# RWKV-style attention and top-1 mixture of experts on one core: R squared up by VectorE, solve in 32x64 tiles, PE and SP queues reordered

## The chip, the cores and the metric

One Trainium2 chip, one of its cores. The metric is the device time of one execution in microseconds (us). The kernel before took 1094.39 us, the median of three runs (1082.82 to 1096.72). Everything is fp32 apart from a few routing tables in bf16.

## The reference, cut to what matters

The input is x of 8 sequences, 512 tokens, 256 channels. The attention layer has 16 heads of 16 channels. Per token it makes, by small and large projections, r, w, k, v, kk, a and a gate g, and runs a delta-rule recurrence per head:

```python
def step(s, inp):
    q_, w_, k_, v_, a_, b_ = inp
    sa = jnp.einsum('bhij,bhj->bhi', s, a_)
    s = s * w_[:, :, None, :] + sa[..., None] * b_[:, :, None, :] + v_[..., None] * k_[:, :, None, :]
    return (s, jnp.einsum('bhij,bhj->bhi', s, q_))
...
x = _layernorm(x + attention(x))
x = _layernorm(x + moe(x))      # 8 experts, 256 -> 1024 -> 256, argmax routing
```

## The kernel before, in words

The recurrence is done in NBLK = 16 blocks of 32 tokens. Inside a block, `scores` (line 646) makes the products of keys and reads, a unit triangular 32x32 matrix per head and sequence has to be inverted, `read_state` (lines 676, 682) gives the right-hand side R and the first part of the output in the PSUM banks `ry0` and `ry1`, `solve` (line 699) multiplies the inverse with R, `update` (716) and `read_out` (728) give the new state and the rest of the output.

256 matrices of a block are inverted on GpSimd (POOL), two halves of 128 partitions packed into one tile, in `invert` (lines 1896, 1903, 1906), one block after the other. They travel through DRAM by SP's queue: `scores_to_pairs(m)` stores the masked scores (scr_n, line 462) and reads them back with a matrix in each partition (467); when POOL is done, `inverse_to_heads(m)` stores the inverse (scr_u, 475) and reads it back in four pieces into `Ux` (486). SP's queue works in order, so each piece waits behind what stands ahead of it. In a body it issues: four loads of tokens (`load_tokens`, 444), the inverse (475, 486), the next input (423), the scores (462, 467), four stores of results (`store_x1`, 452).

The program is software-pipelined by hand: `body(n)` of each engine works on blocks n+2 (first low-rank step), n+1 (projections, decays, keys, scores), n (transposed keys and values, first read of the state), n-1 (R, solve, state, output) and n-2 (normalisation, gate, output projection, token statistics), and n-3 (router logits). Each engine has its own written order. PSUM is shared out by a `Ring`: a list of jobs with the bank of each (`"z@1"`), where a job waits (`wait_empty`) until the readers of the job before it in its bank are done, as named in `freed`. A `Stage` is a semaphore whose values count the steps of an engine, in the written order.

In the kernel before the path of R is: VectorE writes R twice, masked by head parity, into `Rm` (`keep_r`, line 1499, two products of 512 columns); TensorE transposes it (`turn_r`, eight transposes, line 654); ScalarE copies the result into `RT` (`keep_rt`, line 1148, two copies); TensorE multiplies in 64x64 tiles (`solve(m, f)`, 32 matmuls for each half f of the channels), where `Ux` holds the inverse with the other head's places zero; ScalarE and VectorE each copy one half of each result into `XV` (`keep_x` line 1153, `keep_x_odd` line 1505).

PE's body, in order and with lines: R part of read_state (676, 682), keys turned (654), hidden (595), k (561), keys, decay_a_kk (607: z, then a and kk), a filler matmul (769), router and gates (561), ma_mk (607), turn_r (654), project_out (561), solve(1) (699), norms, r (561), keys, v, solve(0) (699), keys and values turned (654), read_out (728), bonus (561), update (716), read_out (728), scores (646), gate_1 and low_1 (561), update, scores, centre_y, read_state, low_2 (579), variance_y, turn_x1. An fp32 matmul leaves two records in the trace, a transpose one.

DVE's chain that ends with the masked keys: keep_r (1499), sum_kk (1411), gated (1529), sum_decays (1391), key_gain (1397, 1399), add_tokens (1539), gain_keys (1415), token_stats (1545 to 1549), keep_x_odd (1505), key_exponent (1403, 1405), normed_kk (1452), decay_reads (1443), decay_kk (1474), removal (1458), decay_keys (1420), bonus_terms (1425), keep_x_odd, mask_removal (1467), mask_keys (1436). `scores` waits for the last of these. ACT feeds it: keep_z and keep_a (1009), keep_logits (1196), sigma_of_z, keep_ma, abs_of_z, keep_rt (1148), square_kk, sigma_of_abs, keep_mk, a table load (1015), log_sigma (1097), log_norm (1101), invert_norm (1122).

After the 16 blocks come the routing and 39 expert blocks, which the change does not touch.

## Time and profile before

| | |
|---|---|
| median of three runs | 1094.39 us (1082.82 to 1096.72) |
| profiled execution, its own time | 1087.63 us |
| its span, first to last instruction | 1085.4 us |
| TensorE clock granted, mean over the span | 0.974 |
| attention blocks | POOL's first inversion starts at 51.6 us, the last of the 16 at 679.4 |

The profile is of one execution. A row of the timeline gives start, duration, engine, line, operation, output and inputs, and how many records were merged; in brackets how long the engine had been idle before it and who ended that. PE is TensorE's matmuls, PEld its weight loads, DVE VectorE, ACT ScalarE, POOL GpSimd, SPq the DMA issues of SyncE. "issue" is idle time for which the profile shows no wait. PEclk is the granted clock as a share of the full one.

### The profile page before, as it was taken

Reading aid. Unit: us, or ns where it says so; the run is one execution under the profiler, and the core shown is the slowest. Engines: PE = TensorE matmul, PEld = TensorE weight load, DVE = VectorE, ACT = ScalarE, POOL = GpSimd, SP = SyncE. Lnnn points to the kernel's source line nnn. Section 1 sums busy time; section 2 is a strip of 40 time slices with the busy share of each in tenths; the row PEclk is TensorE's granted clock in tenths of the full one; section 3 lists DMA queues with packets and bytes.
Section 4 is the critical chain, followed back from the end, with each engine's and each line's share of the span. In section 5 each row is a group of like instructions: output and inputs, shape, how many; then the busy total and the mean of one; then the engine's idle time right before and its main releaser. Section 6 shows DMA issues by size and latency. Waiting matters only on the chain.

```text
span 1085.4 us, 42536 instructions
## 1 busy us (share of the span) xinstructions
PE 1010.8 (93%) x16804; PEld 833.9 (77%) x16805; DVE 777.0 (72%) x1777; ACT 542.0 (50%) x1113; POOL 614.4 (57%) x1135
## 2 busy tenths in 40 slices
PE   8898999999999999999999999499899999999995
PEld 5676777787777787777777777477799888989894
DVE  4776788788887887888788777157467666666663
ACT  4475677686685685776766766122122222222220
POOL 1088786787687885876867868820223232333321
PEclk9999999999999999999999999689999999999998
DMA  4113224234134133243242242828555454545430
GB/s 110 42 20 79 72 43 99 58 56 110 40 73 109 27 86 87 37 99 82 41 100 59 54 101 44 234 63 289 182 182 181 148 185 150 189 144 182 150 125 4
DMA packets 208752, 112.15 MB, mean 103 GB/s; under 512 B 172364, under 2 KB 192080, under 8 KB 208208
## 3 DMA queue, kind: packets, MB, share of 16 engines
q1 hardware_dynamic: 202208, 100.90, 34.4%
q0 software_dynamic: 3744, 8.40, 2.3%
q8 instruction: 122, 2.00, 0.8%
q10 hardware_dynamic: 2640, 0.54, 0.3%
q14 instruction: 38, 0.31, 0.1%
HBM read 85.55 MB, written 26.08 MB: 103 GB/s over the span
## 4 chain that ended last, share of the span: by engine, by line
PE 78%; DMA 7%; DVE 6%; issue 5%; ACT 1%; SPq 1%; POOL 1%; DVEq 1%; POOLq 0%; ACTq 0%
PE bank L561 19%; PE bank L950 12%; PE bank L963 9%; PE bank L646 6%; PE bank L699 6%; PE bank L654 5%; PE ry L963 4%; PE bank L607 3%; PE ry L676 2%; PE ry L728 2%; PE bank L716 2%; DMA arena<-scr_n 2%; DMA scr_n<-arena 2%; DMA arena<-scr_u 2%; DVE arena L1489 1%
## 5 line engine op out<-in xcount | busy, mean ns | idle before, releaser
L1906 POOL TENSOR_TENSOR arena<-arena 128x30 f32<-128x30 f32 (+14 forms) x480 | 263.5, 549 | 37.6
L561 PE MATMUL bank<-arena 128*128 128x256 f32 (+2 forms) x992 | 266.5, 406 | 5.9 <-DVE arena L1405 2.5
L1903 POOL TENSOR_TENSOR arena<-arena 128x30 f32<-128x30 f32 (+14 forms) x480 | 249.9, 521 | 36.4
L561 PEld LDWEIGHTS bank<-arena 128*128 128x128 f32 x992 | 172.7, 196 | 50.9 <-issue 24.7
L950 PEld LDWEIGHTS bank<-arena 128*128 128x128 f32 x1248 | 146.9, 194 | 5.5 <-issue 2.7
L950 PE MATMUL bank<-arena 128*128 128x128 f32 x1248 | 147.4, 277 | 3.1 <-DVE arena L1812 2.5
L1489 DVE TENSOR_TENSOR arena<-bank,arena 128x512 f32<-128x512 f32 x128 | 79.5, 682 | 32.8 <-PE bank L646 32.8
L1293 ACT ACTIVATE arena<-arena 128x1 f32<-128x1 f32 x39 | 11.5, 295 | 177.2 <-DVE arena L1766 177.2
L963 PE MATMUL bank<-arena 128*128 x416 | 96.4, 385 | 0.0
L1937 POOL COPY arena<-arena 128x1 int32 (+1 forms) x39 | 7.1, 183 | 146.2 <-DVE arena L1830 146.2
L963 PEld LDWEIGHTS bank<-arena 128*128 128x128 f32 x416 | 76.9, 190 | 14.4 <-issue 4.8
L699 PEld LDWEIGHTS bank<-arena 64*64 64x64 f32 x2048 | 65.3, 140 | 24.2 <-issue 16.7
L654 PE MATMUL bank<-arena 128*128 128x128 f32 x560 | 80.9, 281 | 2.0 <-issue 0.9
L699 PE MATMUL bank<-arena 64*64 64x32 f32 x2048 | 68.5, 224 | 14.2 <-DMA arena<-scr_u 12.1
L654 PEld LDWEIGHTS bank<-arena 128*128 128x128 f32 x560 | 64.9, 143 | 19.3 <-issue 13.6
L646 PE MATMUL bank<-arena 32*128 32x64 f32 x2048 | 69.0, 275 | 9.4 <-issue 8.5
L1931 POOL DMA_INDIRECT arena<-scr_x,arena x39 | 41.2, 1056 | 61.1 <-POOL arena L1929 30.4
L646 PEld LDWEIGHTS bank<-arena 32*128 32x128 f32 x2048 | 63.8, 188 | 13.7 <-issue 11.5
L1380 DVE SCALAR_TENSOR_TENSOR bank<-bank,arena 128x256 f32<-128x256 f32 x128 | 56.1, 483 | 22.4 <-PE bank L579 22.4
L1896 POOL MEMSET arena<- 128x32 f32 x16 | 2.5, 157 | 121.1 <-DMA arena<-scr_n 121.1
L1812 DVE TENSOR_SCALAR arena<-bank,arena 128x128 f32<-128x128 f32 x156 | 44.0, 344 | 23.1 <-issue 18.0
L1939 POOL DMA_INDIRECT out_dram<-arena x39 | 39.8, 1021 | 34.9 <-DVE arena L1796 20.8
(174 smaller groups left out, 1799.2 us busy)
## 6 DMA issues: line engine op xcount, KB each, us to landing
arena<-in_W SPq DMA_DIRECT2D x47, 1024.0 KB, 5.0
scr_n<-arena SPq DMA_DIRECT2D x64, 128.0 KB, 3.0
arena<-scr_n SPq DMA_DIRECT2D x16, 512.0 KB, 3.9
scr_u<-arena SPq DMA_DIRECT2D x16, 512.0 KB, 2.9
arena<-scr_u SPq DMA_DIRECT2D x62, 128.0 KB, 2.8
arena<-in_xTp SPq DMA_DIRECT2D x32, 132.0 KB, 4.1
arena<-in_x SPq DMA_DIRECT2D x64, 64.0 KB, 2.1
scr_x<-arena SPq DMA_DIRECT2D x64, 64.0 KB, 2.5
```

What stands on the lines that cost most here:

```text
L561: mm = pe.matmul(ring.tile(m, name)[0:rows, to], lhsT, rhs, start=(i == 0), stop=(i == len(terms) - 1))
L646: mm = pe.matmul(ring.tile(m, f"sc{f}{p}")[:, b * 2 * TB:(b + 1) * 2 * TB], bkm[r, f * B + b, :], aq[m % 2][r, f * B + b].rearrange("p x t ...
L654: mm = pe.transpose(ring.tile(m, name)[:, i * P:(i + 1) * P], src, ident)
L699: mm = pe.matmul(ring.tile(m, f"x{f}")[x, at:at + 32], Ux[m % 2][x, f, p, k].rearrange("p h t -> p (h t)"), RT[f][x, k, 32 * p:32 * p + 32 ...
L950: mm = pe.matmul(hidT_ps[t // 4][:, (t % 4) * P:(t % 4 + 1) * P], W1[s][:, k, t * P:(t + 1) * P], xnT[:, k, :], start=(k == 0), stop=(k == ...
L963: mm = pe.matmul(y_ps[s][:, 0:D], hidT[s][:, t, :], W2f[:, bass.ds(e * (FT * D) + t * D, D)], start=(t == 0), stop=(t == FT - 1))
L1380: xm_ok.inc(m, f"{g}{h}", STT(out=part, in0=part, scalar=prm(f"maa{g}", h), in1=dx[:, h], op0=ALU.add, op1=ALU.mult))
L1489: score.inc(m, name, TT(sc[m % 2][:, f, p].rearrange("p k e x t -> p (k e) (x t)"), ring.tile(m, name)[:, :].rearrange("p (b n) -> p b n", ...
L1812: relu_dve.inc(str(t), nc.vector.tensor_scalar(hidT[s][:, t], hidT_ps[1][:, (t - 4) * P:(t - 3) * P], b1f[:, bass.ds(e * FT + t, 1)], 0.0, ...
L1903: inv_ok.inc(f"m{s}", TT(t, U[:, 0:s, s:s + 1].broadcast_to(shape), U[:, s:s + 1, s + 1:TB].broadcast_to(shape), ALU.mult))
L1906: inv_ok.inc(f"a{s}", TT(U[:, 0:s, s + 1:TB], U[:, 0:s, s + 1:TB], t, ALU.add))
L1931: nc.gpsimd.indirect_dma_start(out=xg[:, s], out_offset=None, in_=x_rows, in_offset=bass.IndirectOffsetOnAxis(ap=index, axis=0), bounds_ch ...
```

## The change

- R: VectorE transposes the 32x32 squares of R straight from `ry0` and `ry1` into `Rs` (two transposes of 256 columns). `Rm`, `RT`, turn_r and keep_rt are gone.
- The inverse lies in DRAM and in `Ux` by pairs of heads on 32 partitions, dense; four loads as before, of the same size. The solve multiplies 32x64 tiles: for each pair row w and bank a or b, one matmul of 32 rows of R gives both heads, and the wanted one is picked afterwards.
- keep_x: VectorE takes three products with a 0/1 mask (bank a even and odd, bank b odd, 64x512 each), ScalarE two scaled copies of 64x256 (bank b even).
- PE: gates ahead of decay_a_kk, a and kk ahead of z, ma_mk ahead of the router; solve(0) right behind project_out, then norms, then solve(1), all ahead of r. The second half waits for the first by a semaphore, `half_solved`.
- ACT: a ahead of z, logits behind abs. DVE: gated ahead of sum_kk; all three products of keep_x behind key_exponent.
- SP: the inverse's store goes out first in the body, the token loads behind it (while it lands), the x1 stores of the block before after the inverse's loads.
- The ring's banks are dealt anew: among others v1 moves from bank 4 to 3, ma to 4, g to 4, wo and ss to 0.
- One more load at the start (`head_mask`, 128x34). The four products that mask the keys (1436, 1467) are not touched by the diff.

```diff
-        Rm_flat = take(NB // 2 * P)
-        RT = [take(4 * P).rearrange("p (k n) -> p k n", k=4) for _ in range(HALF)]
+        Rs = take(NB * TB).rearrange("p (e g i) -> p e g i", e=2, g=NB // 2)
+        head_mask = take(TB + 2)
...
-        nd = nc.dram_tensor("scr_n", (HALF, PAIRS, 4, 2, 2 * TB, TB), F32, kind="Internal").ap()
+        nd = nc.dram_tensor("scr_n", (PAIRS, 4, HALF, 2, 2 * TB, TB), F32, kind="Internal").ap()
...
-        ring = Ring(banks, [(0, "bk00@5"), (1, "h@2 k@3"), (0, "bk01@2"), (1, "z@1 a@4 kk@5"), (-3, "logit@2"),
-                            (-2, "g@0"), (1, "ma@5 mk@2"), (-1, "rt0@3 rt1@4"), (-2, "wo@0"), (-1, "x1@1"),
-                            (1, "ss@0 r@4"), (0, "bk11@5"), (1, "v@2"), (-1, "x0@3"), (0, "bk10@5 v0@1 v1@4"),
+        ring = Ring(banks, [(0, "bk00@5"), (1, "h@2 k@3"), (0, "bk01@2"), (-2, "g@4"), (1, "a@5 kk@3 z@1 ma@4 mk@2"),
+                            (-3, "logit@3"), (-2, "wo@0"), (1, "ss@0"), (-1, "xa@1 xb@3"), (1, "r@4"),
+                            (0, "bk11@5"), (1, "v@2"), (0, "bk10@5 v0@1 v1@3"),
...
             def inverse_to_heads(m):
                 sp.dma_start(ud, Up[m % 2].rearrange("p r c -> p (r c)")).then_inc(u_out, 16)
                 if m == last:
                     load_tokens(last)
+                elif m and m - 1 < last - 1:
+                    load_tokens(m - 1)
                 sp.wait_ge(u_out, (m + 1) * 16)
-                for e in range(2 if m < last else 1):
-                    for h in range(2):
-                        at_row = 64 * (1 - e) + TB * h
-                        sp.dma_start(Ux[m % 2][at_row:at_row + TB, :, :, :, h, :], u_rows[e, h]).then_inc(u_in, 16)
+                for p in range(PAIRS if m < last else 2):
+                    sp.dma_start(heads_of(m, p), u_rows[p]).then_inc(u_in, 16)
             def body(n):
-                if has(n - 2) and n - 2 < last - 1:
-                    load_tokens(n - 2)
                 if has(n - 1):
                     inverse_to_heads(n - 1)
+                if has(n - 3) and n <= last:
+                    store_x1(n - 3)
...
-            def solve(m, f):
-                ring.wait_empty(pe, m, f"x{f}")
-                chain_act.wait(pe, m, f"rt{f}")
-                pe.wait_ge(u_in, (m + 1) * 64)
-                for k in range(B // 2):
-                    for p in range(PAIRS):
-                        for e in range(2):
-                            x, at = x_rows_of(e), k * P + 32 * p
-                            mm = pe.matmul(ring.tile(m, f"x{f}")[x, at:at + 32], Ux[m % 2][x, f, p, k].rearrange("p h t -> p (h t)"),
-                                           RT[f][x, k, 32 * p:32 * p + 32], start=True, stop=True)
+            def solve(m, w):
+                if w == 0:
+                    for bank in "ab":
+                        ring.wait_empty(pe, m, f"x{bank}")
+                    chain_dve.wait(pe, m, "re", "ro")
+                    pe.wait_ge(u_in, (m + 1) * 64)
+                else:
+                    pe.wait_ge(half_solved, m + 1)
+                for g in range(NB // 2):
+                    for turn in range(2):
+                        for i, bank in enumerate("ab"):
+                            e, r = (turn + i) % 2, pair_rows(2 * w + i)
+                            at = (w * NB // 2 + g) * 32
+                            mm[bank] = pe.matmul(ring.tile(m, f"x{bank}")[x_rows_of(e), at:at + 32],
+                                                 Ux[m % 2][r, g % 4, g // 4, e].rearrange("p h t -> p (h t)"), Rs[r, e, g, :],
+                                                 start=True, stop=True)
...
-            def keep_rt(m, f):
+            def keep_x(m):
+                ring.wait_full(act, m, "xb")
+                for h in range(2):
+                    chain_act.inc(m, f"xb{h}", A(solution_home(m, 1, 0)[:, :, :, i], solution(m, "xb", 0)[:, :, :, i], ACT.Copy,
+                                                 scale=own_head[x, h:h + 1]))
...
             def keep_r(m):
                 for e, name in enumerate("eo"):
-                    chain_dve.inc(m, f"rm{name}", TT(Rm[:, :, 1 - e], RY[e][:, :, 0, None, :].broadcast_to(shape),
-                                                     odd_even[:, None, :, None].broadcast_to(shape), ALU.mult))
+                    chain_dve.inc(m, f"r{name}", nc.vector.transpose(Rs[:, e], RY[e][:, :, 0]))
+            def keep_x(m, bank, e):
+                ring.wait_full(dve, m, f"x{bank}")
+                chain_dve.inc(m, f"x{bank}{'eo'[e]}", TT(solution_home(m, "ab".index(bank), e), solution(m, f"x{bank}", e),
+                                                         same_head[x_rows_of(e), None, None, :].broadcast_to([P // 2, 2, NB // 2, 32]),
+                                                         ALU.mult))
```

TensorE, before, from the keys turned behind k to the second solve of a middle body (line 607 is decay_a_kk and ma_mk, 654 transposes, 699 solve; matmuls as written, two records each):

```order
L654 MATMUL bank<-arena 128x128 x4
L607 MATMUL bank<-arena 128x256 x6
L769 MATMUL bank<-arena 128x256
L561 MATMUL bank<-arena 128x8 x4
L561 MATMUL bank<-arena 128x256 x2
L607 MATMUL bank<-arena 128x256 x4
L654 MATMUL bank<-arena 128x128 x8
L561 MATMUL bank<-arena 128x256 x4
L699 MATMUL bank<-arena 64x32 x32
```

The same place after (618 is decay_a_kk and ma_mk, 666 transposes, 714 solve, 572 the other projections):

```order
L666 MATMUL bank<-arena 128x128 x4
L572 MATMUL bank<-arena 128x256 x2
L618 MATMUL bank<-arena 128x256 x10
L789 MATMUL bank<-arena 128x256
L572 MATMUL bank<-arena 128x8 x4
L572 MATMUL bank<-arena 128x256 x4
L714 MATMUL bank<-arena 64x32 x32
L572 MATMUL bank<-arena 128x512
L714 MATMUL bank<-arena 64x32 x32
L572 MATMUL bank<-arena 128x256 x4
```

The eight transposes of turn_r are gone, the gates stand two matmuls ahead of a, kk and z, and both halves of the solve stand around norms.

VectorE, before, from the products of keep_r to the second copy of the solution (1499 keep_r, 1529 gated, 1505 keep_x_odd, 1403 and 1405 key_exponent, 1452 normed_kk):

```order
L1499 TENSOR_TENSOR arena<-ry,arena 128x8x64 x2
L1411 TENSOR_TENSOR arena<-bank,arena 128x512
L1529 SCALAR_TENSOR_TENSOR arena<-arena,bank 128x256 x2
...
L1549 BN_AGGR arena<-arena 128x2 x2
L1505 COPY arena<-bank 64x4x128
L1403 SCALAR_TENSOR_TENSOR arena<-arena 128x512
L1405 SCALAR_TENSOR_TENSOR arena<-arena,bank 128x512
L1452 SCALAR_TENSOR_TENSOR bank<-bank,arena 128x512
...
L1425 TENSOR_TENSOR arena<-bank,arena 128x512
L1505 COPY arena<-bank 64x4x128
```

The same place after (1506 keep_r, 1535 gated, 1510 keep_x, 1411 and 1413 key_exponent, 1460 normed_kk):

```order
L1506 STREAM_TRANSPOSE arena<-ry 128x256 x2
L1535 SCALAR_TENSOR_TENSOR arena<-arena,bank 128x256 x2
L1419 TENSOR_TENSOR arena<-bank,arena 128x512
...
L1555 BN_AGGR arena<-arena 128x2 x2
L1411 SCALAR_TENSOR_TENSOR arena<-arena 128x512
L1413 SCALAR_TENSOR_TENSOR arena<-arena,bank 128x512
L1510 TENSOR_TENSOR arena<-bank,arena 64x2x8x32 x3
L1460 SCALAR_TENSOR_TENSOR bank<-bank,arena 128x512
```

Three products stand between key_exponent and normed_kk, where before one copy stood ahead of key_exponent and one far behind normed_kk.

SP's DMA queue, before, one turn (467 scores read back, 452 x1 stores, 444 token loads, 475 inverse stored, 486 inverse read back, 423 next input):

```order
L467 DMA arena<-scr_n 128x1024
L452 DMA scr_x<-arena 32x2x256 x4
L444 DMA arena<-in_x 32x2x256 x4
L475 DMA scr_u<-arena 128x1024
L486 DMA arena<-scr_u 32x32x32 x4
L423 DMA arena<-in_xTp 128x8x33 x2
```

After (479, 487, 456, 498, 464, 435 are the same steps as 467, 475, 444, 486, 452, 423):

```order
L479 DMA arena<-scr_n 128x1024
L487 DMA scr_u<-arena 128x1024
L456 DMA arena<-in_x 32x2x256 x4
L498 DMA arena<-scr_u 32x32x32 x4
L464 DMA scr_x<-arena 32x2x256 x4
L435 DMA arena<-in_xTp 128x8x33 x2
```

The store of the inverse moves past eight issues, its loads past four.

## Rows read from the trace of the kernel before

**Rows 1.** The page: busy time, share of the span and instructions

```profile
PE 1010.8 (93%) x16804; PEld 833.9 (77%) x16805; DVE 777.0 (72%) x1777; ACT 542.0 (50%) x1113; POOL 614.4 (57%) x1135
```

**Rows 2.** POOL: starts of the inversions (first and last), then its timeline

```profile
L1896 POOL MEMSET arena<- x16: 154/158/162, 51.6 to 679.4; 128x32 f32 x16
...
511.36 0.16 POOL L1896 MEMSET arena<- 128x32 f32 x1 [5.98 <-DMA arena<-scr_n]
...
548.15 0.24 POOL L1906 TENSOR_TENSOR arena<-arena 128x30 f32<-128x30 f32 x1
```

**Rows 3.** Windows: stretch, busy PE, PEld, DVE, ACT, POOL, PEclk, DMA share, GB/s

```profile
506.25:548.85 42.60, 41.17 (x921) 32.79 (x921) 34.12 (x61) 29.58 (x56) 32.40 (x61) 0.96 0.31 68
533.54:537.00 3.46, 2.03 (x63) 1.92 (x64) 1.96 (x3) 2.49 (x5) 3.15 (x5) 0.99 0.02 5
537.00:540.30 3.30, 3.30 (x16) 2.64 (x13) 2.48 (x4) 0.70 (x3) 2.91 (x6) 0.50 0.00 0
...
168.30:634.60 466.30, 445.54 (x10121) 353.08 (x10120) 379.98 (x661) 325.26 (x606) 355.64 (x672) 0.99 0.33 71
```

**Rows 4.** Timeline of PE in the body from 506.25 to 548.85

```profile
506.25 1.09 PE L676 MATMUL ry<-arena 32*32 32x64 f32 x64
...
517.29 1.09 PE L654 MATMUL bank<-arena 128*128 128x128 f32 x8
518.22 1.89 PE L561 MATMUL bank<-arena 128*128 128x256 f32 x8
520.04 2.06 PE L699 MATMUL bank<-arena 64*64 64x32 f32 x64
...
533.63 0.89 PE L646 MATMUL bank<-arena 32*128 32x64 f32 x23
535.86 1.64 PE L646 MATMUL bank<-arena 32*128 32x64 f32 x41 [1.34 <-issue]
537.43 3.43 PE L561 MATMUL bank<-arena 128*128 128x256 f32 x8
```

**Rows 5.** Timeline of DVE in the same body

```profile
512.34 1.28 DVE L1499 TENSOR_TENSOR arena<-ry,arena 128x512 f32<-128x512 f32 x2
...
516.34 0.87 DVE L1529 SCALAR_TENSOR_TENSOR arena<-arena,bank 128x256 f32<-128x256 f32 x2 [1.66 <-PE bank L561]
...
520.22 0.69 DVE L1539 TENSOR_TENSOR arena<-bank,arena 128x512 f32<-128x512 f32 x1 [0.48 <-PE bank L561]
...
522.37 0.65 DVE L1505 COPY arena<-bank 64x512 f32<-64x512 f32 x1
...
524.50 0.70 DVE L1452 SCALAR_TENSOR_TENSOR bank<-bank,arena 128x512 f32<-128x512 f32 x1
...
529.08 0.68 DVE L1505 COPY arena<-bank 64x512 f32<-64x512 f32 x1 [0.47 <-PE bank L699]
...
530.88 1.93 DVE L1436 TENSOR_TENSOR arena<-arena 128x512 f32<-128x512 f32 x2
```

**Rows 6.** Timeline of ACT in the same body

```profile
512.95 0.84 ACT L1009 ACTIVATE arena<-bank,arena 128x256 f32<-128x256 f32 x2 [0.22 <-PE bank L607]
515.37 0.18 ACT L1196 ACTIVATE arena<-bank 128x16 f32<-128x16 f32 x1 [1.58 <-PE bank L561]
...
522.29 0.63 ACT L1097 ACTIVATE arena<-arena 128x512 f32<-128x512 f32 x1
```

**Rows 7.** Timeline of SP's DMA issues at the next body's start

```profile
550.01 0.34 SPq L467 DMA_DIRECT2D arena<-scr_n  x1
...
555.12 0.37 SPq L475 DMA_DIRECT2D scr_u<-arena  x1
557.81 2.22 SPq L486 DMA_DIRECT2D arena<-scr_u  x4
```

**Rows 8.** Timeline of PE: the solve of the next and of the last block

```profile
563.93 2.06 PE L699 MATMUL bank<-arena 64*64 64x32 f32 x64 [1.22 <-DMA arena<-scr_u]
...
724.63 3.92 PE L699 MATMUL bank<-arena 64*64 64x32 f32 x128
```

160 lines of the change are left out of this document (77 added, 83 removed), and 2 rows, old and new, of the table ring.

## The prediction

> **What bounds the kernel now.** I read the page first. PE is busy for 93% of the span, the next engine for 72% [rows 1], so the eye goes to PE; but a share says nothing of what an edit is worth in a stage. So I went on to the windows and the timelines.
>
> The 16 attention blocks take most of the time. POOL starts its first inversion at 51.6 and its last at 679.4 us [rows 2]: 627.8 / 15 = 41.9 us for a block. Eleven middle bodies, from 168.30 to 634.60, take 466.30, so 42.39 each, with PE busy for 445.54 [rows 3]: 20.76 / 11 = 1.89 us idle in a body. I follow one body, from 506.25 to 548.85, and give places in it as offsets from 506.25.
>
> On PE the first half of solve starts at 13.8, right behind project_out, and scores at 27.4 [rows 4]. In the scores there is a gap of 1.34 that no wait explains. From 537.00 to 540.30, just behind this gap, the granted clock is 0.50, which is 1.2 GHz of 2.4; ahead of it PE was busy for 2.03 of 3.46 us [rows 3]. The eight matmuls of gate_1 and low_1 that fell into it took 3.36 us (to 540.79), where the eight of project_out took 1.82 [rows 4]: 1.54 us lost.
>
> DVE is the engine to look at beside PE. Its last product of masked keys ends at 530.88 + 1.93 = 532.81, offset 26.6 [rows 5], 0.8 ahead of the scores that wait for it. From add_tokens at 14.0 to there I find one wait of 0.47 between the rows shown, so this stretch is nearly full; it is fed by ACT, whose logarithm ends at 522.92, offset 16.7 [rows 6]. So PE has about 0.8 us in hand over DVE at the scores. What is taken off PE ahead of the scores beyond that turns into a wait, unless DVE's own chain gets shorter too.
>
> The third loop is POOL's. An inversion takes from 511.36 to 548.39, 37.0 us, and ahead of it POOL had waited 5.98 for the scores' loads [rows 2]. Its result was ready at 548.39 but SP stored it only at 555.12, behind the x1 stores and token loads; the loads of it were issued from 557.81 [rows 7] and PE waited 1.22 us for them at 563.93 [rows 8]. In most other bodies this wait is small.
>
> **PE, ahead of the scores.** Eight transposes go: they occupy 517.29 to 518.22, 0.93 us [rows 4]. Each half of solve holds 64 records. In 64x64 tiles they take 522.03 - 520.04 = 1.99 us, 31 ns each. For 32x64 tiles the trace has no row. The nearest ones are these 31 ns and the 32x32 tiles of read_state, 64 records in 1.09 less about 0.1 of drain, some 15 ns [rows 4]. The new shape has four tiles in turn instead of two, so I take 16 ns, 1.0 us per half; the bounds are 0.9 and 2.0. Both halves together save 2.0 us. The clear first half starts at 13.8 - 0.93 = 12.9, ends at 13.9, norms (two records of 512 columns, half the columns of project_out's 1.82) takes 1.0 with its start, and the second half ends at 15.9. With 0.93 + 2.0 saved PE would reach the scores at 27.4 - 2.9 = 24.5.
>
> **DVE and ACT.** keep_r is two products of 512 columns in 1.28 us [rows 5]; now two transposes of 256. No transpose on DVE is in this trace. Between nothing and 1.3 us each they change nothing behind them: DVE waited 1.66 us for the gate's bank [rows 5], and gated, now with its bank filled earlier, takes that place. I take 0.4 each, as a 256-column product of gated (0.87 for two). The Trainium skill gives a price: "VectorE: DVE Perf Modes", section "The three transpose paths", has 311 ns for a 128x128 bf16 transpose on VectorE, so for 256 columns an estimate of 0.62; the sum would be the same by it, since the slack covers it.
>
> What feeds DVE moves both ways. z's two copies began at 512.95, offset 6.7; two groups of matmuls now stand ahead of z (a with kk, and the gates, 1.0 each), so they begin at 8.7 and end at 9.5. Before, ACT then waited 1.58 for the logits [rows 6]; this wait goes, since a comes first. From the logits' end at 515.55 to the logarithm's end ACT needed 7.4 us. Less a's copies, which now stand ahead (0.7), keep_rt (0.5) and a wait of 0.6 for ma, plus the logits (0.2), 5.8 are left: the logarithm ends at 15.3, with a margin 15.5, 1.2 earlier. add_tokens follows project_out at 13.0 instead of 14.0; from it to keep_x_odd DVE took 522.37 - 520.22 = 2.15 [rows 5], to 15.2. key_exponent then runs from 15.5 to 17.0. Then come the three new products of 64x512: by the copy of the same shape 0.65 to 0.68 each, overlapped 1.9 in all, where one copy stood. normed_kk starts at 18.9, against 524.50, offset 18.25, before. From it to the end of the masked keys it was 532.81 - 524.50 = 8.3, with the second copy (0.6) and its wait (0.47) in it: 7.25 without. So the masked keys end at 26.2, with small hand-over delays 26.3: **only 0.3 earlier than before**. This is the term that decides. PE, ready at 24.5, waits about 1.8 us.
>
> ACT has 1.2 us of keep_rt and 1.2 of keep_x less, and two scaled copies of 64x256 more (0.4 each). v1's bank is now one that scores needs, so scores waits for ACT's copy of v1 too; with ACT lighter by 1.6 us I place its end at 25.7, 0.6 ahead of the masked keys. Where this cover is gone it costs what ACT is late.
>
> **Behind the scores.** From 533.63 to the next body's start it was 15.22, less the 1.34 gap and the 1.54 of low clock: 12.3. low_1 waits for the first kept score in its bank; DVE, now with its mix products behind the keys and the scores close behind them, reaches that 0.4 later in relation to PE. I take 12.7. A body free of disturbances is 26.3 + 12.7 = 39.0 (to 0.1).
>
> **Gaps and clock.** Of 1.89 us idle per body before, what falls ahead of the scores is swallowed by the new wait, what falls behind is not; the gap of this body starts in the scores. I keep 0.75 of it. Four of the eleven bodies show a stretch of low clock as in rows 3; with the new wait ahead of the scores I take one in 45 of 100 bodies, 0.7 us. Sum: 39.0 + 0.75 + 0.7 = 40.45, against 42.39: 1.94 less in a body.
>
> On the clock the Trainium skill speaks for the change: "TensorE: Matmul & The Clock Gate", section "HAM oscillation", has the throttle return in long idle waits, such as for DMA. By that rule a wait of 1.8 us costs nothing, and the sum would be 39.75 a body. The trace disagrees: 0.50 was granted behind a gap of 1.34 [rows 3].
>
> **SP and POOL.** The inverse's store passes eight issues: from 555.12 to 550.35 + 0.05, 4.7 us earlier [rows 7]. The token loads stand between it and its loads, but four of them took at most 2.7 us, and the store's landing, 557.81 - 555.12 = 2.7, covers them. Its loads then land about 8.8 us behind the store (issue at 557.81, wait ended at 563.93: 6.1 behind that), at offset 10.4 of the body after, against a solve that now needs them at 12.9. For shorter bodies this holds down to POOL's side: scores read back at 4.7 to 5.1, inversion 37.0, landing 8.8, is 50.9 from a body's start, and the solve is at 12.9 of the next: bodies shorter than 38.0 would wait. I count 0.2 us of waits won in the mean, already in the 1.94. x1 is needed only at the end; storing it later costs nothing while tokens' loads still come by 13.0, and they go out at about 2 to 5.
>
> **The sum.** Bodies 1 to 14 gain 14 x 1.94 = 27.2. Bodies -1 and 0 are padded with filler matmuls and wait for first inversions: nothing. In the last block 128 records of solve took 3.92 us [rows 8] and now about 2.0, but three products replace one copy behind it: 0.7 won. Routing and experts stay. 1087.63 - 27.9 = 1059.7 against the profiled execution's own time, which lies 6.8 below the median of the runs (1094.39). The saving off the median would be 1066.5. I say 1063.
>
> **Rivals.**
> *All of PE's saving counts.* If DVE's chain is not what scores waits for (its three products fit into holes, ACT is earlier than I place it), each body saves 0.93 + 2.0 + 0.2 = 3.1: 14 x 3.1 + 0.7 = 44, so 1044 to 1047. For it: PE is busy 445.54 of 466.30 [rows 3]. Against: the masked keys ended only 0.8 ahead of the scores, and three products now stand in front of them.
> *Nothing is won.* DVE's chain comes out 1 us longer (each product or the logarithm half a microsecond late, or the second half of solve still at 2.0 us, so that the first product waits for it at 17.9), and gaps and low clock stay: bodies of 41.7 to 42.2, 0.2 to 0.7 less: 1077 to 1091, say 1082. For it: DVE gets 0.6 us more work where it is full. This also covers the case that the change doesn't do what it says, tiles of 32x64 that overlap no better than 64x64.
> *Slower by the clock.* PE's new wait ahead of each scores brings low clock in each body, not in four of eleven, and it stays down while the scores and projections behind it run. One stretch costs 1.54. If three follow each other in a body, 39.0 + 0.75 + 4.6 = 44.4, 2.0 more than before: 1087.6 + 28 = 1116. It decides from two such stretches a body on (39.75 + 3.1 = 42.8). For it: rows 3. Against: gaps of 1.3 did this only in some bodies, and the stretch ended by itself after 3.3 us.
>
> **How the numbers follow.** Forecast 0.49, with a range of its own of 1052 to 1074; all of PE 0.17; nothing 0.26; slower by the clock 0.08. About 2% is what a measurement of this kernel tells from no change, here 1072.5 and 1116.3. Faster by more: 0.17 and 0.41 of the forecast's 0.49, 0.58. Within: 0.08 of the forecast's and 0.26, 0.34. Slower: 0.08. The range of 1042 to 1085 leaves out the clock's case and an edge on either side.
>
> **What would show it.** Right, if in the profile after: bodies of 40 to 41 us; the solve's 64 records in about 1.0 us; an idle time of PE of 1 to 2 us ahead of scores that the masked keys end; normed_kk at 18.9 behind R; SP's store of the inverse right behind the scores' load, and no wait for scr_u at solve. Wrong, if scores starts at 24.5 without a wait (then the time is near 1045), if 64 records still take 2.0 us, if another bank (v1, lo1) ends PE's waits, or if the low clock shows in each body.

## The result, and the profile after

The changed kernel took 1077.78 us (median of four runs, 1070.33 to 1079.46), the kernel before beside it 1093.45 (1082.82 to 1096.72): a ratio of 0.9876, 95% interval 0.9831 to 0.992. It is 1.2% faster, 15.7 us, where 1063 (2.8% under 1093.45) was forecast; the direction and the range held, the size did not. The profiled execution took 1079.2 us, span 1077.2, 8.2 less than before's span. It lies 1.4 above its median where before's lay 5.8 below its own, so the two traces show about half of the difference of the medians. In the comparisons below the ratios leave out executions more than 1.5% above the fastest of their kernel, while the medians include them, so that the two can differ by some us.

The page of the changed kernel, part 1, answers to [rows 1]:

```profile
PE 982.2 (91%) x16676; PEld 799.1 (74%) x16677; DVE 779.8 (72%) x1793; ACT 519.5 (48%) x1081; POOL 610.9 (57%) x1135
```

PE is busy for 28.6 us less, but the span fell by 8.2 only. The starts of the solves, which each block has one of, show where. In the table s1 is the solve of block 1, and so on; low clock is the sum of stretches with a granted clock of 0.50.

| stretch of the span | before | after | difference |
|---|---|---|---|
| start to s1 | 140.0 (low 3.4) | 143.2 (13.6) | +3.2 |
| s1 to s13, 12 bodies | 508.6 (13.6) | 491.0 (17.0) | -17.6 |
| s13 to s15 | 76.0 (27.3) | 76.8 (32.2) | +0.8 |
| s15 to first expert matmul | 47.3 (0.0) | 54.1 (15.6) | +6.8 |
| experts to the end | 313.5 (12.5) | 312.1 (9.3) | -1.4 |

The middle gained, 42.38 to 40.92 us a body, and both ends gave some of it back. Windows of the changed kernel, columns as in [rows 3] (the eleven middle bodies, then one of them):

```profile
172.30:620.50 448.20, 420.71 (x10037) 325.05 (x10039) 381.24 (x672) 309.87 (x584) 354.25 (x675) 0.98 0.34 74
499.50:540.60 41.10, 38.45 (x914) 30.04 (x913) 33.93 (x62) 28.13 (x54) 31.20 (x57) 0.96 0.35 74
```

Here a body has 40.75 us, PE is idle for 27.5 / 11 = 2.5 us of it, 0.6 more than before; DVE's work per body is the same as before (34.7 against 34.5 us). The body from 499.50, offsets from there. Timeline of PE, answering to [rows 4]:

```profile
509.85 2.78 PE L572 MATMUL bank<-arena 128*128 128x8 f32 x16
512.57 1.13 PE L714 MATMUL bank<-arena 32*64 32x32 f32 x64
513.63 1.12 PE L572 MATMUL bank<-arena 128*128 128x512 f32 x2
514.68 1.13 PE L714 MATMUL bank<-arena 32*64 32x32 f32 x64
...
522.53 1.10 PE L572 MATMUL bank<-arena 128*128 128x256 f32 x4 [0.62 <-DVE arena L1433]
523.72 0.75 PE L736 MATMUL bank<-arena 128*32 128x32 f32 x64
524.33 0.76 PE L748 MATMUL ry<-arena 128*32 128x32 f32 x64
526.99 2.30 PE L658 MATMUL bank<-arena 32*128 32x64 f32 x64 [1.91 <-issue]
```

Timeline of DVE, answering to [rows 5], and of ACT, answering to [rows 6]:

```profile
505.55 0.77 DVE L1506 STREAM_TRANSPOSE arena<-ry 128x256 f32<-128x256 f32 x2
506.24 0.87 DVE L1535 SCALAR_TENSOR_TENSOR arena<-arena,bank 128x256 f32<-128x256 f32 x2
...
516.40 2.00 DVE L1510 TENSOR_TENSOR arena<-bank,arena 64x512 f32<-64x512 f32 x3
518.33 0.68 DVE L1460 SCALAR_TENSOR_TENSOR bank<-bank,arena 128x512 f32<-128x512 f32 x1
...
523.49 1.70 DVE L1444 TENSOR_TENSOR arena<-arena 128x512 f32<-128x512 f32 x2
```

```profile
514.29 0.63 ACT L1116 ACTIVATE arena<-arena 128x512 f32<-128x512 f32 x1
```

A half of the solve gives way to norms, or to r, 1.06 us after its start, where it took 1.99. The two transposes take 0.77 us together, and gated follows with no wait. The logarithm ends at 514.92, offset 15.4, the masked keys at 525.19, offset 25.7 (26.2 is the median of the bodies). PE would be at the scores at 525.09, and had waited 0.62 for DVE on the way, in front of bonus (L1433 is DVE's product for it). So the two engines arrive together; then a gap that no wait explains puts the scores at offset 27.5.

SP's queue at the start of the next body (540.60), answering to [rows 7], and the waits of PE from 160 to 620 us, in groups (us in total, times, longest):

```profile
542.12 0.34 SPq L487 DMA_DIRECT2D scr_u<-arena  x1
542.55 2.63 SPq L456 DMA_DIRECT2D arena<-in_x  x4
546.17 2.24 SPq L498 DMA_DIRECT2D arena<-scr_u  x4
```

```profile
PE bank L572 <- DVE arena L1433: 8.2, 11, 1.1
PE bank L658 <- issue: 7.8, 10, 1.9
PE ry L694 <- issue: 3.4, 5, 1.0
PE bank L572 <- DVE arena L1497: 3.0, 5, 0.8
PE bank L658 <- DVE arena L1444: 1.6, 6, 0.4
...
PE bank L714 <- DMA arena<-scr_u: 0.8, 2, 0.5
```

PE waits for DVE in every body, for the most part one step ahead of the scores (0.7 us at bonus), and for the inverse almost nowhere.

The ends. Timeline of PE at the first solve and at the last ones, answering to [rows 8]; then the window of low clock around the last, and the one from there to the experts; last, the same stretch of the kernel before (s15 to the first expert matmul):

```profile
99.77 1.50 PE L714 MATMUL bank<-arena 32*64 32x32 f32 x48 [3.39 <-DMA arena<-scr_u]
...
675.58 3.94 PE L714 MATMUL bank<-arena 32*64 32x32 f32 x128 [5.97 <-DMA arena<-scr_u]
...
711.01 4.15 PE L714 MATMUL bank<-arena 32*64 32x32 f32 x128 [4.92 <-DMA arena<-scr_u]
717.36 1.83 PE L748 MATMUL ry<-arena 128*32 128x32 f32 x121 [2.19 <-DVE arena L1510]
```

```profile
709.50:726.60 17.10, 11.84 (x268) 9.63 (x269) 9.93 (x29) 3.31 (x9) 0.74 (x1) 0.50 0.31 85
726.60:765.12 38.52, 35.17 (x195) 28.63 (x193) 19.95 (x60) 4.79 (x10) 3.40 (x4) 1.00 0.72 263
```

```profile
724.63:771.92 47.29, 44.01 (x462) 35.77 (x461) 28.98 (x92) 8.46 (x19) 4.15 (x5) 1.00 0.67 240
```

And the solve of block 14 in the kernel before, a row that the prediction had not read:

```profile
690.00 7.04 PE L699 MATMUL bank<-arena 64*64 64x32 f32 x128 [9.73 <-DMA arena<-scr_u]
```

So both kernels wait for the inverse at the solve of block 14, 9.73 us before and 5.97 now. At that of block 15, PE came without a wait and at full clock before; now it is there sooner than the inverse, waits 4.92 us, and works at 0.50 up to 726.60: the 128 records take 4.15 us, in tiles that should be faster, where the old ones took 3.92.

Not all of this is POOL's own time. POOL's and SP's rows around the inverse of block 14, PE's in the scores of block 15, and windows of low clock there and behind the first solve:

```profile
664.32 0.24 POOL L1913 TENSOR_TENSOR arena<-arena 128x30 f32<-128x30 f32 x1
668.80 0.15 POOL L1903 MEMSET arena<- 128x32 f32 x1 [4.24 <-DMA arena<-scr_n]
```

```profile
664.59 0.44 SPq L514 DMA_DIRECT2D arena<-in_mats  x1
...
666.98 0.43 SPq L517 DMA_DIRECT2D arena<-in_b1T  x1
667.52 0.38 SPq L487 DMA_DIRECT2D scr_u<-arena  x1
```

```profile
649.33 1.44 PE L658 MATMUL bank<-arena 32*128 32x64 f32 x41 [1.36 <-issue]
...
653.07 3.69 PE L658 MATMUL bank<-arena 32*128 32x64 f32 x64
```

```profile
99.77:108.70 8.93, 8.93 (x138) 6.67 (x139) 4.77 (x7) 4.65 (x8) 7.93 (x13) 0.50 0.17 26
651.50:661.70 10.20, 10.20 (x261) 7.76 (x260) 6.37 (x12) 3.54 (x7) 8.87 (x18) 0.50 0.30 50
```

The inverse of block 14 is ready at 664.56, but its store goes out at 667.52, behind three loads for the routing that both kernels issue between these bodies (`load_routing`): 2.9 of the 5.97 us. And the last inversion starts late. Behind the gap of 1.36 us the granted clock was 0.50 for 10.2 us from 651.5, with PE busy throughout; the second half of the scores of block 15 took 3.69 us in it, and POOL could start on them only at 668.80, 34.6 us behind s13, where the kernel before took 30.8.

### The profile page after: what moved, and what is told of

It reads as the page before. It is cut to its first block, busy times and chain, and to the rows that moved or that the text cites. A ratio compares the mean times of both kernels' runs of the same rounds, so it can differ in the third digit from the quotient of the medians.

```text
span 1077.2 us, 42188 instructions
## 1 busy us (share of the span) xinstructions
PE 982.2 (91%) x16676; PEld 799.1 (74%) x16677; DVE 779.8 (72%) x1793; ACT 519.5 (48%) x1081; POOL 610.9 (57%) x1135
## 4 chain that ended last, share of the span: by engine, by line
PE 61%; DVE 12%; POOL 9%; DMA 8%; issue 7%; ACT 2%; SPq 1%; DVEq 1%; ACTq 0%; POOLq 0%
PE bank L572 14%; PE bank L969 12%; PE bank L982 9%; PE bank L658 5%; POOL arena L1913 5%; POOL arena L1910 4%; PE ry L982 4%; PE bank L714 3%; PE bank L618 3%; DMA scr_u<-arena 2%; DMA scr_n<-arena 2%; PE ry L688 2%; PE bank L666 2%; DMA arena<-scr_u 1%; DVE arena L1497 1%
## 5 line engine op out<-in xcount | busy, mean ns | idle before, releaser
L572 PE MATMUL bank<-arena 128*128 128x256 f32 (+2 forms) x992 | 274.9, 412 | 21.3 <-DVE arena L1433 10.8
L572 PEld LDWEIGHTS bank<-arena 128*128 128x128 f32 x992 | 174.1, 198 | 60.8 <-issue 19.6
L969 PEld LDWEIGHTS bank<-arena 128*128 128x128 f32 x1248 | 145.2, 192 | 5.8 <-issue 3.0
L969 PE MATMUL bank<-arena 128*128 128x128 f32 x1248 | 145.9, 275 | 3.2 <-DVE arena L1819 2.5
L1497 DVE TENSOR_TENSOR arena<-bank,arena 128x512 f32<-128x512 f32 x128 | 79.4, 681 | 24.5 <-PE bank L658 24.5
L982 PEld LDWEIGHTS bank<-arena 128*128 128x128 f32 x416 | 76.9, 190 | 14.4 <-issue 4.9
L658 PE MATMUL bank<-arena 32*128 32x64 f32 x2048 | 71.6, 282 | 12.4 <-issue 9.2
L658 PEld LDWEIGHTS bank<-arena 32*128 32x128 f32 x2048 | 66.2, 194 | 17.1 <-issue 15.3
L666 PE MATMUL bank<-arena 128*128 128x128 f32 x432 | 61.9, 278 | 3.6 <-DVE arena L1510 1.6
L666 PEld LDWEIGHTS bank<-arena 128*128 128x128 f32 x432 | 51.5, 143 | 18.0 <-issue 12.0
L714 PEld LDWEIGHTS bank<-arena 32*64 32x64 f32 x2048 | 37.9, 149 | 33.8 <-issue 23.8
L1316 ACT ACTIVATE arena<-bank,arena 128x128 f32<-128x128 f32 x156 | 44.5, 368 | 25.3 <-PE bank L969 25.3
```

Of the source, the lines that this page charges most:

```text
L572: mm = pe.matmul(ring.tile(m, name)[0:rows, to], lhsT, rhs, start=(i == 0), stop=(i == len(terms) - 1))
L658: mm = pe.matmul(ring.tile(m, f"sc{f}{p}")[:, b * 2 * TB:(b + 1) * 2 * TB], bkm[r, f * B + b, :], aq[m % 2][r, f * B + b].rearrange("p x t ...
L666: mm = pe.transpose(ring.tile(m, name)[:, i * P:(i + 1) * P], src, ident)
L714: mm[bank] = pe.matmul(ring.tile(m, f"x{bank}")[x_rows_of(e), at:at + 32], Ux[m % 2][r, g % 4, g // 4, e].rearrange("p h t -> p (h t)"), R ...
L969: mm = pe.matmul(hidT_ps[t // 4][:, (t % 4) * P:(t % 4 + 1) * P], W1[s][:, k, t * P:(t + 1) * P], xnT[:, k, :], start=(k == 0), stop=(k == ...
L982: mm = pe.matmul(y_ps[s][:, 0:D], hidT[s][:, t, :], W2f[:, bass.ds(e * (FT * D) + t * D, D)], start=(t == 0), stop=(t == FT - 1))
```

## The experiments

Theory A: the middle bodies gained what DVE and ACT's chain allows, and the rest was lost at both ends, where PE, now earlier, waits for the inverse and pays for it again by the clock. Theory B: the chain itself is longer than forecast. Theory C: it is chance, gaps that move with the program's code. Differences below are between medians unless said otherwise; each ratio is to the kernel before run beside it. Only the next four experiments (again, fillers, narrowed, SP's old order) ran beside the changed kernel; the others are set against it by way of their ratios.

**The changed kernel again.** 

> The changed kernel again, on the chip of the next three, so that they can be set against it. In its first profile a middle body took 40.75 us against 42.39 before, as the forecast's chain gives (scores start at 26.4 of the body, 26.3 was forecast); but the first two bodies were 3.2 us later and 6.6 us were lost between the last solve and the first expert block, where the clock was low for 17 us. Theory A (what was won in the middle is given back at the two ends, where PE waits for the inverse and the clock falls): the same again, 12 to 20 us faster than before, middle bodies 40.4 to 41.0. Rival B (that profile was an odd one; the ends cost nothing): 25 to 30 us faster.

Measured: 1079.89, ratio 0.9892 (0.9848 to 0.9937). Body 40.94, last solve to experts 54.9, and again low clock (13.7 us) in the scores of block 15, with the last inversion 36.9 us behind s13: what the first trace showed repeats. Its profiled execution took 1087.25, 7.4 above the median, so it shows the losses larger than they mostly are.

**Fillers at both ends.**

```diff
+                if n == 1 or n == last:
+                    ring.wait_empty(pe, n - 1, "xa")
+                    keep_busy(6 if n == 1 else 11, ring.tile(n - 1, "xa"))
                 if has(n - 1) and n - 1 < last:
                     solve(n - 1, 0)
...
-                    keep_busy(2, idle_ps)
+                    keep_busy(12, idle_ps)
...
+                if n == last + 1:
+                    keep_busy(4, route_ps)
```

> Filler matmuls where PE waits for the inverse: 6 ahead of the first solve, 11 ahead of the solve of block 14, 12 in place of 2 ahead of that of block 15, 4 behind it. Nothing that anyone waits for is made earlier. Theory A: the low-clock stretches at both ends go or shrink from about 50 us in all to under 25, the first two bodies come back by 1 to 2 us and the stretch from the last solve to the first expert block by 4 to 6: 4 to 8 us faster than the changed kernel. Rival C (the ends are late by the waits alone, the clock has no part in it): no change, or slower by up to 2 us through fillers that run over.

Measured: 1071.08, ratio 0.9822 (0.9778 to 0.9866), 8.8 less than the changed kernel beside it. Low clock behind s13 fell from 51.3 to 17.0 us, last solve to experts from 54.9 to 50.4. The work added is 31 matmuls, and yet the time falls. The two traces exaggerate, since that of this kernel is of its fastest execution (1065.55). Against the first trace of the changed kernel s1 comes 2.1 us earlier (141.1), s13 to s15 takes 1.7 less and the stretch to the experts 3.7 less, but 6.1 us stand in the twelve middle bodies (40.41 us each), in which the edit adds nothing. By the ratios the gain is 7.6 us.

**DVE's three products narrowed.** `keep_x` on DVE takes 4 of 32 columns in blocks 2 to 14; the rest of the masking is left out.

> VectorE's three products of keep_x take 4 of 32 columns in blocks 2 to 14, so the kernel leaves out most of the masking of the solution there; nothing else is moved. This takes about 1.4 us out of VectorE's chain ahead of the masked keys. Theory D (that chain is what scores waits for): the masked keys end 1.4 earlier, scores starts 0.5 to 1.0 earlier (then ScalarE's copy of v1, which ends at 25.9, or PE itself comes last), bodies 0.4 to 1.0 us shorter, 5 to 12 us in all. Rival E (PE's own work sets the body, its waits are only where it happens to pause): under 2 us.

Measured: 1067.73, ratio 0.9776 (0.9719 to 0.9833), 12.2 less. The three products take 0.61 us in place of 2.00, and the masked keys end at offset 25.3; the scores still start at 26.3 (26.4 in the changed kernel), now behind ACT's copy of v1, which ends at 25.8. Timeline of DVE in this kernel:

```profile
510.26 0.61 DVE L1511 TENSOR_TENSOR arena<-bank,arena 64x64 f32<-64x64 f32 x3
510.79 0.68 DVE L1460 SCALAR_TENSOR_TENSOR bank<-bank,arena 128x512 f32<-128x512 f32 x1
```

The middle bodies have 40.57 us, 0.35 to 0.37 less for 1.39 us taken out of the chain. So the chain is on the path, but ACT is close behind DVE, as the 0.6 us of cover in the prediction said, and only about 4 of the 12.2 us come from these bodies. In the profiles 3.3 to 5.0 us stand ahead of s1, where the edit changes nothing, and 3.8 to 6.0 between s13 and s15, where this kernel has no low clock ahead of the last inversion.

**SP's old order in the changed kernel; SP's new order alone in the kernel before.** In the first `load_tokens` is ahead of `inverse_to_heads` again, `store_x1` behind `scores_to_pairs`' loads; in the second the kernel before gets only SP's part of the diff.

> The changed kernel with SP's old order: x1 stores and token loads ahead of the inverse's store. Theory F (the new order is needed now, since the first solve stands 2 us earlier in the body than before): the inverse lands at about 15 of the body instead of 10.5, PE waits about 2 us at each solve, the second half ends at 18, keep_x and all behind it come 0.8 to 1.0 later: 10 to 16 us slower than the changed kernel, that is about as slow as before. Rival G (the inverse was never late by more than its 0.2 us in the mean): under 3 us slower.

> The kernel before with SP's new order and nothing else: the inverse's store goes out first, token loads behind it, x1 stores behind its loads. The undoing of it in the changed kernel cost 18 us, more than the 16 us that the whole change brings. Theory F (the new order is worth much only together with the earlier solve; before, PE waited for the inverse 0.2 us in a body and at three places at the ends): 2 to 7 us faster than before, from the waits of 9.7 and 1.2 us at the last blocks. Rival H (SP's order is the whole gain, the rest of the change brings nothing): 12 to 18 us faster than before.

Measured: the first 1098.21, ratio 1.0052 (1.0015 to 1.0089), 18.3 more than the changed kernel beside it by the medians and 17.5 by the ratios, bodies of 42.31; the second 1092.22, ratio 0.9997 (0.9964 to 1.003), bodies of 42.70. PE's waits of the first from 160 to 640 us:

```profile
PE bank L656 <- issue: 6.1, 8, 1.2
PE bank L712 <- DMA arena<-scr_u: 5.6, 5, 1.8
PE bank L712 <- issue: 4.3, 2, 3.2
```

The new order is worth all of the gain in one kernel and nothing in the other. Twelve bodies of 42.31 instead of 40.94 are 16.4 us. PE's waits for the inverse show 5.6 of them directly; 4.3 more at the solve have no wait that the profile shows. The delay runs on through the solve: the masked keys end at 27.6 of a body in the mean, where it was 26.3. Alone in the kernel before, the new order cut the wait at s14 from 9.73 to 6.38 us, but the 2 to 7 us that this was expected to bring did not come. Only where the solve stands earlier in the body does the inverse come last.

**z ahead of a and kk.** On PE and ACT, and in the order of the stage.

```diff
-                from_hidden(m, [[("a", 0, slice(64, 96), hid), ("kk", 0, slice(96, 128), kkh)]])
                 from_hidden(m, [[("z", 2, slice(0, P), hid)]])
+                from_hidden(m, [[("a", 0, slice(64, 96), hid), ("kk", 0, slice(96, 128), kkh)]])
```

> The changed kernel with z ahead of a and kk again, on TensorE and ScalarE. In the two bodies at the start, where no gates stand ahead, a and kk wait 0.4 to 0.8 us for ScalarE's copy of k (its bank is kk's now), and the first inversion starts at 53.1 instead of 51.6, the second at 92.6 instead of 90.3. Theory A: the first inversion starts at 51.6 to 52.0 again, the second at 90.5 to 91.5; in a middle body nothing changes, since ScalarE makes z and a one after the other: 0 to 3 us faster. Rival: the order of a and z sets ScalarE's logarithm, then bodies move by 0.5 us either way and the time by 6.

Measured: 1072.82, ratio 0.9855 (0.9805 to 0.9906). s1 is at 140.3, as before the change, and bodies have 40.23. In the changed kernel a and kk wait at the start for ACT's copy of k, since kk lies in k's bank; with z first they don't. PE of the changed kernel, and of this one:

```profile
55.27 1.98 PE L618 MATMUL bank<-arena 32*128 32x256 f32 x11 [0.40 <-ACT arena L1084]
```

```profile
53.65 2.09 PE L618 MATMUL bank<-arena 128*128 128x256 f32 x12
```

The wait is gone, and the first inversion starts at 52.1 instead of 53.1. How much of s1's 3.2 us it explains is not shown: s1 was at 143.2 and 144.9 in the two traces of the changed kernel, and at 139.9 in the kernel with the narrowed products, whose program is the same up to there. Most of the gain stands in the middle bodies, 0.7 us each, as the rival allowed and theory A did not: the logarithm ends 0.3 us earlier, at offset 15.2, and part is low clock, 6.8 us in the twelve instead of 17.0. The interval overlaps with those of the changed kernel (0.9831 to 0.992, 0.9848 to 0.9937).

**Fillers ahead of the scores.** Two, in the bank of the first score, in bodies 1 to 14.

> The changed kernel with two filler matmuls (0.92 us) ahead of the scores in the bodies 1 to 14, where PE waits for the masked keys. Theory D (PE waits there about 1 us in a body, split into 0.7 ahead of bonus and 0.3 ahead of scores): fillers that fit into what is left of the wait cost little, 0.3 to 0.6 us a body, 3 to 8 us slower, unless they keep the clock up; if a short wait there is what brings the low clock in the middle (17 to 24 us of it in two profiles), that falls to under 10 us and the two cancel: 3 us faster to 4 us slower. Rival E (PE sets the body): 0.92 us in each of 14 bodies, 13 us slower.

Measured: 1072.45, ratio 0.9837 (0.9789 to 0.9884), an interval that again overlaps with those of the changed kernel. Low clock in the middle 6.8 us, as expected; bodies of 40.75, which is 2 us less in twelve. That 0.92 us of fillers a body cost nothing rules out rival E, that PE's work alone sets the body.

**Router ahead of ma and mk, alone and with those fillers.** `router(n - 3)` and its filler stand ahead of `ma_mk(n + 1)` again.

> The changed kernel with the router (and the filler matmul ahead of it) back in front of ma and mk. Theory D (the chain z, ma, mk on ScalarE, logarithm, key_exponent, three products, masked keys sets the scores): ma's bank is filled 1.5 us later, ScalarE waits 0.7 us for it, the logarithm ends at 16.1 instead of 15.5 and the masked keys 0.6 later; bodies 0.4 to 0.6 us longer, 5 to 9 us slower. Rival E (PE sets the body): nothing, under 2 us.

> The changed kernel with router and its filler back ahead of ma and mk (which alone made bodies of 42.98 and 54 us of low clock in the middle), and two fillers ahead of the scores. If the clock amplifies a delay of ACT's chain (a longer wait ahead of the scores brings low clock), the fillers take most of the low clock away: bodies of 41.5 to 42.0, 10 to 14 us faster than router first alone, ratio 0.990 to 0.994. If the chain alone makes the bodies long, the fillers give nothing: bodies of 42.8 to 43.2, ratio 1.002 to 1.006.

Measured: alone 1096.39, ratio 1.0042 (1.0 to 1.0085), bodies of 42.98 with 54.4 us of low clock in the twelve; with the fillers 1085.75, ratio 1.0001 (0.9969 to 1.0033), bodies of 41.85 with 20.4. Alone, the logarithm ends 0.9 us later (offset 16.4), the body 2.1; PE's waits from 160 to 640:

```profile
PE bank L572 <- DVE arena L1433: 14.7, 11, 1.9
```

A delay of 0.9 in the chain made the wait at bonus 1.3 instead of 0.7 us a body. The clock can account for the rest: 54.4 - 17.0 = 37.4 us more at half speed are 3.1 in a body, which costs up to 1.6. The fillers shorten no chain, and in the profile they still took half of it back. How large the amplification is stays uncertain. The profile without fillers is of one of its longer executions (1099.23; four of the ten took 1086 to 1089), and the fillers won 4.5 us by the ratios, where 10 to 14 were expected; the two intervals overlap.

**Together, and in the kernel before.** The third has the fillers of the second experiment ahead of its solves, in the bank `x1`, without the four behind the last.

> The changed kernel with all three edits that each gave 7 to 9 us: z ahead of a and kk, two filler matmuls ahead of the scores in bodies 1 to 14, and the fillers at the first and the last two solves. If the three gain from different places (start and bodies, gaps of the bodies, end), they add up in part: period of the middle bodies 40.1 to 40.5, low clock to the last solve's experts under 20 us, last solve to first expert matmul 50 to 51 us; the time about 1060 to 1066, ratio 0.973 to 0.978. If they all only remove the same low clock, the best single one is the floor: 1068 to 1072, ratio 0.981 to 0.984.

> The changed kernel with z ahead of a and kk and the fillers at the ends, without the fillers ahead of the scores. If the fillers ahead of the scores cost bodies their own time (two matmuls of 0.47 us in a wait of 0.7 to 1.8 us) and give back only in bodies with low clock, this is equal to the kernel with all three, within 3 us. If the gaps ahead of the scores are what starts the low clock, it is 3 to 7 us slower than with all three.

> The kernel before with the same fillers at the ends (6 ahead of the first solve, 11 ahead of the solve of block 14, 12 in place of 2 ahead of the last). Theory: the changed kernel lost 6.8 us between its last solve and the experts to waits and low clock that the kernel before hasn't; there PE waited little, so fillers only stand in PE's way: 0 to 4 us slower than before, ratio 1.000 to 1.004. Rival: the fillers are a gain of their own that any kernel has, which says nothing of the change: 4 to 9 us faster, ratio 0.992 to 0.996.

Measured: all three 1074.65, ratio 0.9874 (0.9818 to 0.993); z and ends 1070.3, 0.9853 (0.9802 to 0.9904); the kernel before with fillers 1098.55, 1.0111 (1.0067 to 1.0155). Nothing adds up: bodies have 41.21 and 40.77 us, longer than with z first (40.23) or the end fillers (40.41) alone. The fillers are not a gain that any kernel has: before the change they cost 11 us, more than expected. From s14 to s15 there are 37.9 us instead of 34.6, since PE had no wait at s15 to fill; 6 us stand in middle bodies that the edit doesn't touch (42.86). The expectation was wrong to say that PE waited little there: it waited 9.73 at s14, and filling that gave nothing.

**Code moved, nothing else.** Five or ten matmuls of 8 columns more in body 0, ahead of a wait; and the fillers at both ends once more beside them.

> The changed kernel with five matmuls of 8 columns more (0.17 us each by the router's row) behind the fillers of body 0, where PE then waits 3.39 us for the first inverse anyway. They can change no body behind it but by moving the program's later code on in memory. If the gaps that the profile puts down to issue (7.8 us ahead of matmuls of the scores in eleven bodies) are set by where code stands, they fall in other places, and the period of the middle bodies leaves 40.92 by 0.2 to 0.6 us either way, the time by 2 to 8 us. Rival: the period is set by the chain of DVE and ACT alone: 40.8 to 41.0, time within 2 us of 1078 to 1080.

> The same with ten such matmuls. If code placement counts, the period of the middle bodies differs from that with five by 0.2 to 0.6 us, in no order that the number of matmuls explains; by the rival it is 40.8 to 41.0 again.

> The changed kernel with the fillers at its first and its last two waits once more, beside the two shifted kernels on one chip. If its 8.8 us came from the waits at the ends, it is again 50 to 51 us from the last solve to the first expert matmul with under 20 us of low clock there, and 6 to 10 us faster than the shifted kernels; if from a lucky placement of the middle bodies, the profile has the same 40.4 period (the code is the same) and the ends are where the difference isn't.

Measured: 1082.64, ratio 0.9936 (0.9905 to 0.9967), and 1082.88, ratio 0.9941 (0.9904 to 0.9978), with bodies of 41.00 and 40.91; the fillers 1069.99, ratio 0.9859 (0.9824 to 0.9895), with bodies of 40.48 and 49.3 us from last solve to experts. For these two shifts theory C falls for the body: the gaps ahead of the scores went from 7.8 us to 6.0 and 10.0, the period stayed. Both are 3 to 5 us slower than the changed kernel by the medians and 5 to 7 by the ratios; up to 4.4 of it stand ahead of s1 (145.0 and 147.6 for 143.2). The gain of the fillers holds: 12.7 us against the shifted kernels by the medians, 8.4 to 8.9 by the ratios. Timeline and window of its last solve:

```profile
699.23 5.34 PE L789 MATMUL bank<-arena 128*128 128x256 f32 x24
704.50 2.35 PE L714 MATMUL bank<-arena 32*64 32x32 f32 x128
706.78 1.99 PE L789 MATMUL bank<-arena 128*128 128x256 f32 x8
```

```profile
704.50:753.80 49.30, 43.98 (x469) 35.48 (x468) 29.70 (x89) 8.11 (x19) 4.14 (x5) 1.00 0.65 232
```

No wait, full clock, and 2.35 us for the 128 records that took 4.15. With a ratio of 0.9822 and 0.9859 in its two comparisons it is the best confirmed version; z first (0.9855) and the fillers ahead of the scores (0.9837) can't be told from it. Its interval overlaps a little with that of the changed kernel beside it the first time, and not with those of the two shifted ones.

## Why the prediction was right and wrong

- *The solve, 1.0 us a half for 2.0*: right. The pitch from one half to the next step is 1.06, which is 17 ns a record.
- *DVE's transposes, 0.4 each, without effect*: right, 0.77 for both.
- *ACT's chain, logarithm at 15.5; products 1.9; normed_kk at 18.9; masked keys at 26.3*: right to 0.3: 15.5, 2.0, 19.15, 26.2 in the median. This was the term called decisive. Narrowing the products made the bodies 0.35 us shorter, delaying the logarithm made them longer.
- *PE waits 1.8 us ahead of the scores*: half right. PE waits for the same chain one step earlier, at bonus, 0.7 us a body, and arrives at offset 25.6 in the body shown, not 24.5. I had put no name to that step's input, DVE's product behind normed_kk.
- *A body of 40.45*: nearly, 40.92 between solves. Behind the scores 14.3 us stood where 12.7 + 0.75 + 0.7 = 14.15 was summed; another part is gaps ahead of the scores, as the 1.91 in the body shown, which I had let the wait swallow. So 1.46 us was gained, not 1.94: 12 x 0.48 = 5.8 us of the miss.
- *Bodies 1 to 14 gain 14 x 1.94*: **the step that failed**, together with the two terms for the ends that follow. The steady gain was carried over to the whole pipeline. Twelve bodies gained. From s13 to s15 the kernel got 0.8 us slower, where 2 x 1.94 was counted, 4.7 us of the miss: these solves wait for the inverse, 5.97 and 4.92 us. The sentence on POOL's side said that bodies shorter than 38.0 us would wait, and was used for the steady state alone; the last bodies have no next block to project, and from s14 to s15 there were 34.6 us already before. A part is the clock and not the change of pace: in the traces of changed kernels where 0.50 was granted around the scores of block 15, s13 to s15 took 75.8 to 79.0 us, in the others 71.5 to 75.1, against 76.1 before.
- *Bodies -1 and 0: nothing*: wrong, +3.2 us. The moved a and kk need a bank that ACT still holds; PE waits, the first inversion starts 1.5 us later, and the first solve waits 3.39 us, with the clock at 0.50. Putting z first took the wait for the bank away; that it also gave back all of the 3.2 is not shown, since s1 moved as much between kernels with the same program up to there.
- *In the last block 0.7 won*: wrong, 6.8 us lost up to the experts, 7.5 of the miss and its largest term. 2.35 us, not 2.0, is what 128 records cost at full clock, and here they ran at half of it. It had 15.6 us of low clock in this stretch, the kernel before none.
- *The sum off the median*: the terms give 28 us, 15.7 were measured. (1063 itself is the mean of this sum off the profiled execution and off the median, and lies 3.5 below the latter.) In the traces the four misses above, 5.8, 4.7, 3.2 and 7.5, make 21.2 of 27.9. The profiles show 17.6 in the middle, and +3.2, +0.8, +6.8 and -1.4 elsewhere, which is 8.2 in sum; the other 7.5 come almost wholly from where the two profiled executions stand to their medians.
- *SP: the inverse goes first, 0.2 us won*: the waits are gone as said (0.8 us in eleven bodies), but its worth was undersized. Taken out of the changed kernel it costs 16 to 18 us; I had priced it against the old body, where it is worth nothing, and not against the new one that needs it.
- *The rivals*: "nothing is won" named a chain 1 us longer; the run with the router first is that case, and it came out at the kernel before's time (ratio 1.0042). "Slower by the clock" did not happen in the middle (17.0 us of low clock in twelve bodies against 13.6), but the mechanism is real: that run had 54.4.

On the clock, the changed kernel waits for a transfer from 706.09 to 711.01 and is granted 0.50 from 709.50 for 17.1 us; at the first solve it waits up to 99.77 and is granted 0.50 from 98.50 for 10.2 us. The Trainium skill, "TensorE: Matmul & The Clock Gate", section "HAM oscillation", has the throttle return in long waits for DMA; at both ends the trace agrees. The prediction weighed it only against the gap of 1.34 us in the middle, where trace and page differ (the 0.50 behind the gap of 1.36 in the scores of block 15 is another such place), and did not ask where the change makes long waits.

What stays open: why the fillers at the ends also shorten the middle bodies, 40.92 to 40.4 and 40.5 in two profiles, and lengthen them in the kernel before; part is low clock (13.7 and 6.8 us in the twelve, for 17.0), the rest was not traced. So about half of what the fillers win is not explained by the ends. Nor was it tried to move `load_routing` behind the store of block 14's inverse, or to bring the last two inversions forward, which would take the waits at the end away instead of filling them.

## What to carry to other kernels

Price a gain per stage, the first and the last ones apart: a body that gets faster in the steady state meets a slow feeder first where the pipeline fills and drains, and what stands in the queue there (here the loads for the next stage) delays that feeder further. When a change moves a consumer earlier, price each edit to its feeder against the new place, not the old; alone it may measure as nothing and still carry all of the gain. And where a wait on TensorE comes out of such a change, look at the granted clock behind it before counting the wait alone: fillers in it were worth 8 to 13 us here, and cost 11 us in the kernel that did not have the last of these waits. One trace can mislead by as much: between kernels with the same program up to s1, s1 moved by 5 us.

## What the hardware showed that was not expected

- Low clock begins in a wait and outlasts it. At the first solve PE was busy without a pause from 99.77 to 108.70, 8.9 us, and was granted 0.50 all the time; the wait before had been 3.39 us. In the scores of block 15 a gap of 1.36 us was followed by 10.2 us at 0.50, with PE busy for all of them.
- A delay can be amplified by the clock: 0.9 us later in ACT's chain went with bodies 2.1 us longer and 54.4 us of low clock against 17.0, in one trace each; two filler matmuls a body brought it to 20.4.
- VectorE transposes 256 fp32 columns of 128 partitions from PSUM, in 32x32 squares, in 0.77 us for two, where one product of 512 columns takes 0.69.
- Single-edit gains of 7 to 9 us by the medians did not add up, and edits elsewhere moved the period of untouched bodies by 0.5 us. Comparisons of under 0.5% between two builds of this kernel say little on one edit.
